# One maximum reduction per head over three key blocks in the causal attention stage

## The chip, the cores and the metric

The kernel runs on one core of a Trainium2 chip. Its time is the device time of the whole program in microseconds (us); a lower time is better. PE is the matrix engine, PEld its weight loads, DVE the vector engine, ACT the scalar engine, POOL the GpSimd engine and SP the engine that issues most transfers.

## The reference

The program applies eight layers to x of shape 16 x 256 x 256 in float32. Each is preceded by a layer norm and added to x. The change touches one of them, the causal self-attention inside the layer L2_ffn, with 16 heads of 16 columns each:

```python
def attention(x, c_attn_w, c_proj_w):
    b, t, c = x.shape
    hd = c // H                       # H = 16, hd = 16
    q, k, v = jnp.split(x @ c_attn_w, 3, axis=-1)
    ...
    att = jnp.einsum('bhqd,bhkd->bhqk', q, k) / jnp.sqrt(jnp.asarray(hd, x.dtype))
    causal = jnp.tril(jnp.ones((t, t), bool))
    att = jnp.where(causal, att, jnp.asarray(-jnp.inf, att.dtype))
    att = jax.nn.softmax(att, axis=-1)
    y = jnp.einsum('bhqk,bhkd->bhqd', att, v)
    y = y.transpose(0, 2, 1, 3).reshape(b, t, c)
    return y @ c_proj_w
...
x = x + attention(layernorm(x, ln1_w), c_attn_w, c_proj_w)
x = x + moe_mlp(layernorm(x, ln2_w), router_w, w1, w2)
```

The softmax needs the maximum over keys of each query of each head. For 256 queries in two tiles of 128, the first tile sees the first 128 keys only, the second all 256. That is three blocks of 128 x 128 scores.

## The kernel before, in words

The function `attention` is called for five attention layers. A call works on 16 units, one batch element of 256 tokens each; the call named a2 holds two layers, first a cross attention (units 0 to 15, a2 in the trace) and behind it the causal self-attention (units 16 to 31, also named a2 in the trace). `stage(u).causal` tells them apart. The tokens, queries, keys and values of several units are in flight at once. A table made by `plan()` gives the order of work for all engines: each period has 16 slots, one for each head, and every engine walks the same table, `PLAN`, and does its own part of each entry. Engines wait for each other by semaphores (`S[name]`).

In slot i of a period, entry `sst` (line 901) makes PE compute the scores of head i of one unit, queries on partitions (`scores`, line 854), into score bank `i % 2`, and interleaved with it the transposed scores of a head of an older unit (`scoresT`, line 866) into one of three other banks. For the causal layer, `diagonal` (line 878) then adds a large negative triangle to the two diagonal blocks. A causal head's scores lie as three adjacent blocks of 128 columns in its bank: queries 0 to 127 against keys 0 to 127, queries 128 to 255 against keys 0 to 127, queries 128 to 255 against keys 128 to 255.

DVE reads the bank and writes the negated maximum of each query into one column of the tile NM (lines 1183 to 1199). For a layer without the causal mask that is one reduction with two outputs (line 1196). For the causal layer there are two reductions a head (line 1193), over 128 and over 256 columns. The second raises the signal `s_max`. PE waits before the scores of head i for `s_max` of head i - 2 (line 907), since there are two score banks. At the change from one unit to the next this goes on: the first head of a unit waits for head 14 of the one before.

In slot 1 of the next period, entry `maxT` (line 979) waits for `s_max` of all 16 heads and transposes the two halves of NM; ACT and DVE split the result into two bfloat16 parts (lines 1110 and 1300), which SP moves into rows of the query tile, so that the transposed scores come out with the maximum subtracted. ACT then takes the exponential (line 1061), and PE multiplies by the values (line 1002).

Between the reductions DVE also does, by the same table: layer-norm statistics (line 1248), the low bfloat16 parts of K and Q (line 1296), the division by the softmax sums (lines 1312 and 1322), the low part of the output (line 1325), the addition to the layer's result (line 1339), and, in the causal units, the router of the following mixture-of-experts layer (statistics at lines 136 to 145, a copy of logits at line 213, the selection at lines 228 to 302 once for each group of units).

Of the kernel before, what the change touches and what calls it, by code (L numbers as in the profile page):

```python
# [4 lines left out]
P = 128  # L5
D = 256
BATCH = 16
SEQ = 256
# [13 lines left out]
F32 = mybir.dt.float32  # L22
# [4 lines left out]
AX = mybir.AxisListType  # L27
ADD, SUB, MUL, MAX, MIN = ALU.add, ALU.subtract, ALU.mult, ALU.max, ALU.min
# [288 lines left out]
def late(u):  # L317
# [3 lines left out]


ATT = ["stats_step", "var_ready", "rstd_ready", "norm_step", "xh_ready", "xs_ready", "ch_ready", "cs_ready", "xT_ps", "xT_sb", "cT_ps", "cT_sb",
       "q_ps", "q_hi", "q_lo", "k_ps", "k_full", "k_hi", "k_lo", "mask_row", "v_ps", "v_sb", "s_ps", "s_max",
       "mT_ps", "m_hi", "m_lo", "st_ps", "p_ready", "pv_ps", "pv_sb", "oT_ps", "recip", "o_ready",
       "o2T_ps", "o2_hi", "o2_lo", "y_ps", "x_done", "x_biased",
       "x_half", "x_joined", "fin_step", "fin_var", "fin_rstd", "fin_n", "fin_max"]
# [13 lines left out]
def attention(nc, g, S, cfg):  # L341

    NH, DH = cfg["heads"], D // cfg["heads"] if "dh" not in cfg else cfg["dh"]
# [11 lines left out]
    stages = [Stage(cfg)] + ([Stage(cfg["then"])] if "then" in cfg else [])  # L355
# [8 lines left out]
    def stage(u):  # L364
        return stages[u // BATCH]
# [8 lines left out]
               k_lo=NB, v_ps=NB, v_sb=NB, s_ps=NH, s_max=NH, st_ps=NH, p_ready=NH,  # L374
# [135 lines left out]
    with ExitStack() as ctx:  # L510
        def sb(name, shape, dt):
            return ctx.enter_context(nc.sbuf_tensor(cfg["name"] + name, shape, dt))
# [10 lines left out]
        QS = sb("QS", [P, RING, CH, GH, SEQ], BF16)  # L523
        KS = sb("KS", [P, RING, CH, GH, SEQ], BF16)
        VA = sb("VA", [P, VRING, 2, NH, VW], F32)
        NM = sb("NM", [P, 2, 2, P], F32)
        MKI = sb("MKI", [P, BATCH * SEQ], I32) if mask else None

        VECS = [sb("VEC%d" % n, [P, 8 + 3 * CK], F32) for n in range(NP_)]
# [67 lines left out]
        with nc.Block() as block:  # L597
# [224 lines left out]
            def _(pe):  # L822
# [64 lines left out]
                for name, u, i, b, before in PLAN:  # L887
# [58 lines left out]
                    elif name in ("q", "k"):  # L946
                        p = u // BATCH
# [29 lines left out]
                                           [wv[:, x, kt, :] for x in range(2)]) for kt in range(KT)])  # L977
                        m.then_inc(S["v_ps"].sem, 1)
                    elif name == "maxT":
                        pe.wait_ge(S["s_max"].sem, S["s_max"].at(u, NH))  # L980
                        take(before)
                        for t in range(2):
                            m = nc.tensor.transpose(misc[:, t * P:t * P + P], NM[:, u % 2, t, :], ident[:])
                        m.then_inc(S["mT_ps"].sem, 1)
                    elif name == "pv":
                        pe.wait_ge(S["p_ready"].sem, S["p_ready"].at(u, (i + 1) * HS))
                        pe.wait_ge(S["v_sb"].sem, S["v_sb"].at(u, NB))
                        take(before)
                        causal = stage(u).causal
                        for t in range(2):  # L990
                            q0 = P if causal and t == 1 else 0
                            for j in range(HS):
                                h = i * HS + j
                                slot = order(h) % 8
                                if wide:
                                    a = (t * HS + j) * W
                                    for kt in range(2):
                                        m = nc.tensor.matmul(misc[:, a:a + VW],
                                                             PT[:, slot, kt * SEQ + t * P:kt * SEQ + t * P + P],
                                                             VA[:, u % VRING, kt, h, :], start=(kt == 0), stop=(kt == 1))  # L1000
                                else:
                                    m = nc.tensor.matmul(misc[32 * j:32 * j + 32, q0:SEQ], VA[:, u % VRING, t, h, :],
                                                         PT[:, slot, t * SEQ:t * SEQ + SEQ - q0],
                                                         start=(t == 0), stop=(t == 1 or causal),
                                                         skip_group_check=causal, tile_position=(0, 32 * j))
                        m.then_inc(S["pv_ps"].sem, 1)
                    elif name == "oT":
                        pe.wait_ge(S["pv_sb"].sem, S["pv_sb"].at(u, (i + 1) * 4 // NO))
                        take(before)
                        for t in range(2):  # L1010
                            for k in range(2):
                                m = nc.tensor.transpose(misc[:, t * 256 + k * P:t * 256 + k * P + P],
                                                        OS[:, 2 * i + k, t * P:t * P + P], ident[:])
                        m.then_inc(S["oT_ps"].sem, 1)
                    elif name == "o2T":
                        pe.wait_ge(S["o_ready"].sem, S["o_ready"].at(u, NO))
                        take(before)
                        for j in range(2):
                            kt = 2 * i + j
                            for t in range(2):  # L1020
                                m = nc.tensor.transpose(misc[:, j * 256 + t * P:j * 256 + t * P + P],
                                                        O[:, t, kt * P:kt * P + P], ident[:])
                        m.then_inc(S["o2T_ps"].sem, 1)
                    elif name == "y" and proj:
                        pe.wait_ge(S["o2_hi"].sem, S["o2_hi"].at(u, NB))
                        pe.wait_ge(S["o2_lo"].sem, S["o2_lo"].at(u, NB))
                        take(before)
                        wo = wos[u // BATCH]
                        for t in range(2):
                            out = misc[:, t * 256:t * 256 + 256]  # L1030
                            m = product3(out, [([oT[:, x, kt, t * P:t * P + P] for x in range(2)],
                                            [wo[:, x, kt, :] for x in range(2)]) for kt in range(CK)])
                        m.then_inc(S["y_ps"].sem, 1)
# [93 lines left out]
            def _(dve):  # L1127
# [32 lines left out]
                for name, u, i, b, before in PLAN:  # L1160
# [22 lines left out]
                    elif name == "sst" and u is not None:  # L1183
# [5 lines left out]
                        col = i if wide else 8 * (i % 2) + i // 2  # L1189
                        bank = ps[:, i % 2, :]  # L1190
                        if stage(u).causal:
                            for t, (lo, hi) in enumerate(((0, P), (P, P + SEQ))):
                                s_ = nc.vector.tensor_reduce(NM[:, u % 2, t, col:col + 1], bank[:, lo:hi],  # L1193
                                                             AX.X, MAX, negate=True)
                        else:
                            s_ = nc.vector.tensor_reduce(NM[:, u % 2, :, col:col + 1],  # L1196
                                                         bank.rearrange("p (t k) -> p t k", t=2),
                                                         AX.X, MAX, negate=True)
                        s_.then_inc(S["s_max"].sem, 1)
                    elif name == "fin":  # L1200
                        step, h = S["fin_step"], u % 2
                        if u == 0:
# [3 lines left out]
                        for t in range(2):  # L1206
                            s_ = nc.vector.bn_stats(FS6[:, t, :], X[:, 2 * u + t, :])
# [3 lines left out]
                        for t in range(2):  # L1211
                            s_ = nc.vector.bn_aggr(FMV[:, h, t, :], FS6[:, t, :])
# [8 lines left out]
                    elif name == "joined":  # L1221
                        WT = g["WT"]
                        for t in range(2 * u, 2 * u + 2):
                            dve.wait_ge(g["gathered"][t % 4], 32 * (t // 4 + 1))
                            s_ = nc.vector.scalar_tensor_tensor(X[:, t, :], GB[:, t % 4, 0, :], WT[:, 0, t:t + 1],
                                                                X[:, t, :], MUL, ADD)
                        s_.then_inc(S["x_half"].sem, 1)
                        dve.wait_ge(S["x_half"].sem, S["x_half"].at(u, 1))
                        for t in range(2 * u, 2 * u + 2):
                            s_ = nc.vector.scalar_tensor_tensor(X[:, t, :], GB[:, t % 4, 1, :], WT[:, 1, t:t + 1],  # L1230
                                                                X[:, t, :], MUL, ADD)
# [122 lines left out]

def signal_used(n, cfg, q, own_ctx, wide):
    proj, mask, self_att = cfg.get("proj"), cfg.get("mask"), q.self_att
    if n in ("q_moved", "q_sent"):
        return (n == "q_sent") == bool(cfg.get("router"))
    if n in ("o2T_ps", "o2_hi", "o2_lo", "y_ps"):
        return bool(proj)  # L1360
    if n in ("pv_sb", "oT_ps"):
        return not wide
    if n in ("k_full", "mask_row"):
        return bool(mask)
    if n in ("ctx_in0", "ctx_in1"):
        return not self_att
    if n in ("cT_ps", "cT_sb", "ch_ready", "cs_ready"):
        return own_ctx
    if n in ("cT_kept0", "cT_kept1"):
        return cfg.get("keep") is not None  # L1370
    if n in ("fin_step", "fin_var", "fin_rstd", "fin_n", "fin_max"):
        return bool(cfg.get("fin"))
    if n == "x_biased":
        return q.biased
    if n in ("x_half", "x_joined"):
        return bool(cfg.get("gather"))
    return True
# [1182 lines left out]
```

## Time and profile before

| | us |
|---|---|
| median of 3 runs | 3309.73 |
| lowest and highest of them | 3307.66, 3317.76 |
| the profiled execution's own time | 3314.98 |
| its span, first to last instruction | 3313.2 |
| TensorE clock granted, mean over the span | 0.921 of full |

The span belongs to one execution. A row of the trace gives the start or the count, the duration, the engine, the source line and the operation as out<-in with the shapes (partitions x elements). What stands in brackets is the idle time of the engine just before, and what ended it. Busy times of PE include a modelled end of each matmul.

### The profile page before, as it was taken

How to read it: one execution, taken by the hardware profiler on the slowest of the kernel's cores; microseconds unless marked ns; L12 is line 12 of the kernel's file. 1: busy time of each engine (PE TensorE's matmuls, PEld its weight loads, DVE VectorE, ACT ScalarE, POOL GpSimd, SP SyncE). 2: the span in 40 equal slices, each digit the busy share in tenths (PEclk: the TensorE clock that was granted, in tenths of full speed). 3: DMA queues.
4: the chain of work that ended last, by engine and by line, in shares of the span. 5: the costliest groups of instructions: out<-in, count | busy, mean ns of one | idle time of the engine just before them, and what ended most of it. 6: DMA issues, size and time to landing. Idle time of an engine off the chain costs nothing. (4 is left out here: it accounts for less than half of the span.)

```text
span 3313.2 us, 69870 instructions
## 1 busy us (share of the span) xinstructions
PE 2813.2 (85%) x25966; PEld 1896.0 (57%) x26085; DVE 1984.3 (60%) x4625; ACT 1663.2 (50%) x3058; POOL 1137.0 (34%) x1192
## 2 busy tenths in 40 slices
PE   4999686888789999999969999998469958999993
PEld 2554463555346666666635556666269936676672
DVE  4887555888455433433358887787554345555547
ACT  2778342777444444444427776766355513333332
POOL 6653008887000000000043334464400064565513
PEclk8999896999779999999969999999789968999995
DMA  3332002222214000000011211111243233332301
GB/s 115 74 74 60 14 5 90 66 67 68 45 53 147 1 1 1 1 1 1 1 60 58 74 47 51 41 61 56 81 143 97 84 100 79 81 83 63 77 20 51
DMA packets 164743, 189.87 MB, mean 57 GB/s; under 512 B 25968, under 2 KB 136832, under 8 KB 164256
## 3 DMA queue, kind: packets, MB, share of 16 engines
q1 hardware_dynamic: 147520, 143.44, 14.5%
q0 software_dynamic: 16896, 41.97, 4.9%
q8 instruction: 218, 3.57, 0.5%
q14 instruction: 109, 0.89, 0.1%
HBM read 67.09 MB, written 41.42 MB: 33 GB/s over the span
## 5 line engine op out<-in xcount | busy, mean ns | idle before, releaser
L1900 DVE TENSOR_TENSOR f1H<-f1HF,f1H 128x512 bf16<-128x512 f32 x256 | 176.6, 692 | 398.3 <-ACT f1H L1740 398.3
L1695 PE MATMUL ps<-f1w,f1H 128*128 128x256 bf16 x3072 | 379.1, 274 | 0.0
L1673 PE MATMUL ps<-f1xT,f1w 128*128 128x512 bf16 x1448 | 360.3, 384 | 12.1 <-ACT f1H L1740 5.9
L1695 PEld LDWEIGHTS ps<-f1w,f1H 128*128 128x128 bf16 x3072 | 301.8, 98 | 90.8 <-issue 1.7
L1737 ACT ACTIVATE f1HF<-ps 128x512 f32<-128x512 f32 x256 | 152.8, 597 | 333.9 <-PE ps L1673 333.8
L1061 ACT ACTIVATE a2PT<-ps 128x512 f32<-128x512 f32 (+1 forms) x512 | 260.1, 542 | 81.7 <-PE ps L884 58.7
L1673 PEld LDWEIGHTS ps<-f1xT,f1w 128*128 128x128 bf16 x1536 | 148.5, 99 | 152.5 <-issue 18.8
L861 PE MATMUL ps<-a2KS,a2QS 49*128 49x256 bf16 (+1 forms) x1024 | 175.9, 267 | 53.9 <-DVE a2NM L1196 20.9
L1583 POOL TENSOR_TENSOR f1RS<-f1VE,neghalf 128x4 f32<-128x4 f32 x8 | 8.1, 1011 | 578.0 <-DVE f1VE L1883 578.0
L1196 DVE TENSOR_REDUCE a0NM<-ps 128x2 f32<-128x512 f32 x256 | 165.5, 685 | 38.2 <-PE ps L861 37.6
L1196 DVE TENSOR_REDUCE a1NM<-ps 128x2 f32<-128x512 f32 x256 | 165.7, 686 | 37.5 <-PE ps L861 35.9
L1196 DVE TENSOR_REDUCE a2NM<-ps 128x2 f32<-128x512 f32 x256 | 165.7, 686 | 27.7 <-PE ps L861 26.0
L873 PE MATMUL ps<-a2QS,a2KS 51*128 51x256 bf16 (+1 forms) x1024 | 173.2, 264 | 0.2 <-ACT a2PT L1061 0.2
L1061 ACT ACTIVATE a4PT<-ps 128x512 f32<-128x512 f32 x128 | 76.0, 597 | 191.6 <-PE ps L873 191.6
L1193 DVE TENSOR_REDUCE a2NM<-ps 128x1 f32<-128x128 f32 (+1 forms) x512 | 150.4, 350 | 31.1 <-PE ps L884 29.8
L1061 ACT ACTIVATE a1PT<-ps 128x512 f32<-128x512 f32 x256 | 143.0, 595 | 25.3 <-PE ps L873 23.7
L805 POOL DMA_INDIRECT Y<-results,IX x64 | 63.4, 990 | 264.6 <-DMA results<-f2OB 247.5
L861 PEld LDWEIGHTS ps<-a2KS,a2QS 49*128 49x128 bf16 x1024 | 67.3, 95 | 147.3 <-DVE a2NM L1196 48.7
L1740 ACT ACTIVATE f1H<-ps 128x512 bf16<-128x512 f32 x256 | 151.5, 592 | 0.0
L1061 ACT ACTIVATE a0PT<-ps 128x512 f32<-128x512 f32 x256 | 141.5, 593 | 16.9 <-PE ps L873 13.6
L861 PE MATMUL ps<-a4KS,a4QS 128*128 128x256 bf16 (+1 forms) x512 | 126.9, 283 | 17.4 <-DMA a4QS<-a4QH 17.4
L733 POOL TENSOR_TENSOR a2RS<-a2VE,neghalf 128x4 f32<-128x4 f32 x32 | 32.7, 1021 | 310.1 <-DVE a2VE L1267 310.1
(538 smaller groups left out, 7046.0 us busy)
## 6 DMA issues: line engine op xcount, KB each, us to landing
a2KS<-a2KH SPq DMA_DIRECT2D x192, 64.0 KB
a2QS<-a2QH SPq DMA_DIRECT2D x192, 64.0 KB
a4KS<-a4KH SPq DMA_DIRECT2D x96, 128.0 KB
a4QS<-a4QH POOLq DMA_DIRECT2D x96, 128.0 KB, 4.3
slots<-zeros SPq DMA_DIRECT2D x1, 9984.0 KB, 31.9
f2XG<-slots SPq DMA_DIRECT2D x39, 256.0 KB, 2.9
results<-f2OB SPq DMA_DIRECT2D x39, 256.0 KB, 2.1
f1WF<-in_f_w SPq DMA_DIRECT2D x32, 256.0 KB, 2.7
```

The source lines that it names most:

```text
L733: nc.gpsimd.tensor_tensor(RS[:, h], VE[:, h], g["neghalf"][:, 0:4], ALU.pow).then_inc(S["rstd_ready"].sem, 1)
L805: nc.gpsimd.indirect_dma_start(GB[:, t % 4, k, :], None, g["results"][:, :], bass.IndirectOffsetOnAxis(ap=g["IX"][:, k, t:t + 1], axis=0)) ...
L861: m = nc.tensor.matmul(bank[:, at:at + keys], QS[r0:r1, u % RING, ch, gi, t * P:t * P + P], KS[r0:r1, u % RING, ch, gi, 0:keys], start=(ch ...
L873: m = nc.tensor.matmul(bank[:, at:at + SEQ - q0], KS[r0:r1, u % RING, ch, gi, t * P:t * P + P], QS[r0:r1, u % RING, ch, gi, q0:SEQ], start ...
L1061: nc.scalar.activation(PT[:, ic % 8, 0:n_], ps[:, 2 + (uc * NH + ic) % 3, 0:n_], ACT.Exp, scale=scale).then_inc(S["p_ready"].sem, 1)
L1193: s_ = nc.vector.tensor_reduce(NM[:, u % 2, t, col:col + 1], bank[:, lo:hi], AX.X, MAX, negate=True)
L1196: s_ = nc.vector.tensor_reduce(NM[:, u % 2, :, col:col + 1], bank.rearrange("p (t k) -> p t k", t=2), AX.X, MAX, negate=True)
L1673: m = nc.tensor.matmul(ps[:, (u * NCH + i) % 2, :], w1[:, x, kt, i * P:i * P + P], xT[:, half, y, kt, :], start=(j == 0), stop=(j == len(t ...
L1695: m = nc.tensor.matmul(out, H[:, (u * NCH + i) % HR, x, t * P:t * P + P], w2[:, y, i, :], start=first, stop=(f == YC - 1 and j == 2 and no ...
L1737: nc.scalar.activation(HF[:, (u * NCH + i) % 2, :], ps[:, (u * NCH + i) % 2, :], cfg["gelu"], **bias).then_inc(S["h_full"].sem, 1)
L1740: nc.scalar.activation(H[:, (u * NCH + i) % HR, 0, :], ps[:, (u * NCH + i) % 2, :], cfg["gelu"], **bias).then_inc(S["h_hi"].sem, 1)
L1900: nc.vector.tensor_tensor(H[:, (u * NCH + i) % HR, 1, :], HF[:, (u * NCH + i) % 2, :], H[:, (u * NCH + i) % HR, 0, :], SUB).then_inc(S["h_ ...
```

## The change

In the causal layer one reduction a head now covers the three blocks of 128 columns and writes three outputs, so NM has three blocks instead of two in the call a2. After the last head of a unit, DVE waits for its own reductions and takes the elementwise minimum of the blocks 1 and 2 (of negated maxima, 128 x 16) into block 1, and raises a new signal `m_full`. PE's `maxT` waits for `m_full` instead of `s_max` in the causal layer. The reduction of the other layers is the same as before, written with an explicit `0:2`.

```diff
-        NM = sb("NM", [P, 2, 2, P], F32)
+        NM = sb("NM", [P, 2, 3 if any(q.causal for q in stages) else 2, P], F32)
...
                     elif name == "maxT":
-                        pe.wait_ge(S["s_max"].sem, S["s_max"].at(u, NH))
+                        if stage(u).causal:
+                            pe.wait_ge(S["m_full"].sem, S["m_full"].at(u % BATCH, 1))
+                        else:
+                            pe.wait_ge(S["s_max"].sem, S["s_max"].at(u, NH))
...
                         if stage(u).causal:
-                            for t, (lo, hi) in enumerate(((0, P), (P, P + SEQ))):
-                                s_ = nc.vector.tensor_reduce(NM[:, u % 2, t, col:col + 1], bank[:, lo:hi],
-                                                             AX.X, MAX, negate=True)
+                            s_ = nc.vector.tensor_reduce(NM[:, u % 2, :, col:col + 1],
+                                                         bank[:, 0:3 * P].rearrange("p (b k) -> p b k", b=3),
+                                                         AX.X, MAX, negate=True)
                         else:
-                            s_ = nc.vector.tensor_reduce(NM[:, u % 2, :, col:col + 1],
+                            s_ = nc.vector.tensor_reduce(NM[:, u % 2, 0:2, col:col + 1],
                                                          bank.rearrange("p (t k) -> p t k", t=2),
                                                          AX.X, MAX, negate=True)
                         s_.then_inc(S["s_max"].sem, 1)
+                        if stage(u).causal and i == NH - 1:
+
+                            dve.wait_ge(S["s_max"].sem, S["s_max"].at(u, NH))
+                            nc.vector.tensor_tensor(NM[:, u % 2, 1, 0:NH], NM[:, u % 2, 1, 0:NH], NM[:, u % 2, 2, 0:NH], MIN
+                                                    ).then_inc(S["m_full"].sem, 1)
```

The name `m_full` is also added to the list `ATT`, and `signal_used` returns `q.causal` for it.

On DVE, at the change from one causal unit to the next in a period with the router's copy of logits, the order before was (a2oT is the low part of the output, f2G the router's logits; the four reductions are heads 14 and 15, the two behind the copy are head 0 of the next unit):

```order
L1325 TENSOR_TENSOR a2oT<-ps,a2oT 128x512
L1193 TENSOR_REDUCE a2NM<-ps 128x1 x4
L213 COPY f2G<-ps 128x16
L1193 TENSOR_REDUCE a2NM<-ps 128x1 x2
L1248 BN_STATS a2ST<-X 128x6 x2
```

and with the change it is:

```order
L1333 TENSOR_TENSOR a2oT<-ps,a2oT 128x512
L1195 TENSOR_REDUCE a2NM<-ps 128x3 x2
L1206 TENSOR_TENSOR a2NM<-a2NM 128x16
L213 COPY f2G<-ps 128x16
L1195 TENSOR_REDUCE a2NM<-ps 128x3
L1256 BN_STATS a2ST<-X 128x6 x2
```

The minimum (line 1206) stands between head 15 and the copy of logits, and so ahead of head 0 of the next unit; each pair of reductions is one.

On PE, at entry `maxT` of a causal unit, with the signals that each row waits for, the order before was:

```order
L884 MATMUL ps<-tri_t,idh 128x2x128
L983 MATMUL ps<-ident,a2NM 128x128 [waits r_gc,s_max]
L983 MATMUL ps<-ident,a2NM 128x128
L1002 MATMUL ps<-a2PT,a2VA 32x256 [waits xT_sb,v_sb,p_ready]
```

and with the change:

```order
L884 MATMUL ps<-tri_t,idh 128x2x128
L986 MATMUL ps<-ident,a2NM 128x128 [waits r_gc,m_full]
L986 MATMUL ps<-ident,a2NM 128x128
L1005 MATMUL ps<-a2PT,a2VA 32x256 [waits xT_sb,v_sb,p_ready]
```

PE's rows keep their places; only the signal before the transposes differs.

## Rows read from the trace of the kernel before

**Rows 1.** The page, busy time of each engine over the whole span.

```profile
PE 2813.2 (85%) x25966; PEld 1896.0 (57%) x26085; DVE 1984.3 (60%) x4625; ACT 1663.2 (50%) x3058; POOL 1137.0 (34%) x1192
```

**Rows 2.** Busy times by stretch: PE, PEld, DVE, ACT, POOL, clock, DMA share, GB/s.

```profile
1999.00:2325.00 326.00, 302.19 (x4359) 213.49 (x4359) 257.42 (x886) 218.00 (x448) 172.07 (x167) 0.97 0.16 52
```

**Rows 3.** Table of waits from 1999 to 2325: us in total, times, longest.

```profile
PEld ps L861 <- DVE a2NM L1193: 32.0, 86, 2.1
...
PE ps L861 <- DVE a2NM L1193: 15.2, 24, 1.8
```

**Rows 4.** Timeline of weight loads: start, us, operation, idle before and its releaser.

```profile
2083.38 0.09 PEld L861 LDWEIGHTS ps<-a2KS,a2QS 49*128 49x128 bf16 x1 [0.62 <-DVE a2NM L1193]
...
2008.21 0.09 PEld L861 LDWEIGHTS ps<-a2KS,a2QS 49*128 49x128 bf16 x1 [0.41 <-DVE a2NM L1193]
...
2087.32 0.09 PEld L861 LDWEIGHTS ps<-a2KS,a2QS 49*128 49x128 bf16 x1 [0.20 <-issue]
```

**Rows 5.** Timeline of DVE in a steady causal unit.

```profile
2080.34 0.69 DVE L1296 TENSOR_TENSOR a2KH<-ps,a2KH 128x512 bf16<-128x512 f32 x1 [1.19 <-ACT a2KH L1094]
...
2082.71 1.14 DVE L1193 TENSOR_REDUCE a2NM<-ps 128x1 f32<-128x128 f32 x4
2083.77 0.68 DVE L1296 TENSOR_TENSOR a2QH<-ps,a2QH 128x512 bf16<-128x512 f32 x1
```

**Rows 6.** DVE by line and shape: count, busy us, mean ns, idle before.

```profile
L1193 DVE TENSOR_REDUCE a2NM<-ps 128x1 f32<-128x256 f32 x256 | 106.2, 415 | 0.0
L1193 DVE TENSOR_REDUCE a2NM<-ps 128x1 f32<-128x128 f32 x256 | 72.8, 285 | 31.1 <-PE ps L884 29.8 <-issue 0.4
...
L1196 DVE TENSOR_REDUCE a2NM<-ps 128x2 f32<-128x512 f32 x256 | 165.7, 686 | 27.7 <-PE ps L861 26.0
...
L232 DVE TENSOR_REDUCE f2RK<-a2WF 128x64 f32<-128x512 f32 x2 | 1.4, 686 | 0.1
```

**Rows 7.** Timeline of DVE late in the cross-attention units, two heads in a row.

```profile
1993.61 1.29 DVE L1196 TENSOR_REDUCE a2NM<-ps 128x2 f32<-128x512 f32 x2 [0.26 <-PE ps L861]
1994.81 0.25 DVE L1312 RECIPROCAL a2RC<-ps 128x16 f32<-128x16 f32 x1
```

**Rows 8.** Timeline of DVE around the router's selection, and in the last period.

```profile
2160.35 0.61 DVE L1193 TENSOR_REDUCE a2NM<-ps 128x1 f32<-128x128 f32 x2
...
2172.01 0.17 DVE L301 TENSOR_TENSOR f2AB<-f2AB 128x8 f32<-128x8 f32 x1
2172.21 0.17 DVE L302 CAST IX<-f2AB 128x16 int32<-128x16 f32 x1
2172.29 1.15 DVE L1193 TENSOR_REDUCE a2NM<-ps 128x1 f32<-128x128 f32 x4
...
2315.59 3.59 DVE L1193 TENSOR_REDUCE a2NM<-ps 128x1 f32<-128x128 f32 x12
```

**Rows 9.** Timeline of DVE, a dependent pair of statistics and a small product.

```profile
2095.23 0.25 DVE L1257 BATCH_NORM_AGGREGATE a2MV<-a2ST 128x2 f32<-128x6 f32 x2 [0.17 <-DVE a2ST L1248]
...
2096.84 0.41 DVE L1302 TENSOR_TENSOR a2MH<-ps,a2MH 16x256 bf16<-16x256 f32 x1
```

**Rows 10.** Timeline of DVE and of weight loads at a change of causal units.

```profile
2092.32 1.14 DVE L1193 TENSOR_REDUCE a2NM<-ps 128x1 f32<-128x128 f32 x4
...
2093.78 0.62 DVE L1193 TENSOR_REDUCE a2NM<-ps 128x1 f32<-128x128 f32 x2 [0.24 <-PE ps L884]
...
2095.92 0.20 PEld L983 LDWEIGHTS ps<-ident,a2NM 128*128 128x128 f32 x2 [0.16 <-issue]
```

**Rows 11.** Line 721, POOL's clearing of NM: ns min/median/max, start.

```profile
L721 POOL MEMSET a2NM<- x1: 519/519/519, 1667.5 to 1667.5; 128x512 f32 x1
```

**Rows 12.** Busy times by stretch behind the router's selection, columns as in Rows 2.

```profile
2165.00:2170.00 5.00, 2.48 (x30) 1.71 (x32) 4.62 (x23) 1.69 (x4) 1.62 (x2) 1.00 0.24 81
2170.00:2175.00 5.00, 3.91 (x51) 2.58 (x52) 4.36 (x19) 2.35 (x5) 1.47 (x2) 0.65 0.15 52
2175.00:2180.00 5.00, 5.00 (x61) 3.33 (x61) 2.62 (x8) 2.88 (x5) 3.33 (x4) 0.67 0.30 103
```

More of the change, by code:

```diff
@@ L323 @@
 ATT = ["stats_step", "var_ready", "rstd_ready", "norm_step", "xh_ready", "xs_ready", "ch_ready", "cs_ready", "xT_ps", "xT_sb", "cT_ps", "cT_sb",
-       "q_ps", "q_hi", "q_lo", "k_ps", "k_full", "k_hi", "k_lo", "mask_row", "v_ps", "v_sb", "s_ps", "s_max",
+       "q_ps", "q_hi", "q_lo", "k_ps", "k_full", "k_hi", "k_lo", "mask_row", "v_ps", "v_sb", "s_ps", "s_max", "m_full",
        "mT_ps", "m_hi", "m_lo", "st_ps", "p_ready", "pv_ps", "pv_sb", "oT_ps", "recip", "o_ready",
@@ L1356, in signal_used @@
     proj, mask, self_att = cfg.get("proj"), cfg.get("mask"), q.self_att
+    if n == "m_full":
+        return q.causal
     if n in ("q_moved", "q_sent"):
```

## The prediction

> **What bounds the kernel now.** I read the page first: over the whole span PE is busy 85%, DVE 60% [rows 1]. That average says little, since the change touches one stage. The causal units run from 1999 us to 2325 us of the span, and the table by stretches gives that stage alone: PE 302.2 of 326 us (93%), PE's weight loads 65%, DVE 79%, ACT 67% [rows 2]. So PE is nearest to full, with DVE behind it. The table of waits then says how often DVE's maxima hold PE up: matmuls of line 861 sat idle 15.2 us in 24 places for the tile NM, and weight loads of that line 32.0 us in 86 places [rows 3]. Not all of the 32.0 us is loss. After other matmul work line 861 shows a gap of 0.20 us with nothing to wait for the third of [rows 4], and 86 such gaps are 17.2 us; what is really lost to DVE is therefore about 15 us in 326, by both ways of counting. The timeline shows the kinds of place. In a steady unit DVE does the low part of K, a reciprocal, a product and statistics from 2080.34 us on and reaches two waiting score banks only at 2082.71 us [rows 5]; PE, which has two score banks, resumes at 2083.38 us after 0.62 us of idle weight loads [rows 4], 0.06 us after the first head's maxima ended (2082.71 + 0.61). Elsewhere DVE waits for PE.
>
> **What goes and what comes.** 512 reductions go (256 over 128 elements, mean 285 ns, and 256 over 256 elements, mean 415 ns) [rows 6]; 256 reductions over 384 elements and 16 minima of 128x16 come. No matmul, activation, transfer or its order moves. PE's transposes wait for the new signal instead of the maxima.
>
> *One reduction over 384 elements.* No row has it. The two neighbours are 256 elements at 415 ns and 512 elements (two outputs) at 686 ns [rows 6]; halfway is 550 ns. The number of outputs seems free: 64 outputs from 512 elements take 686 ns as well [rows 6]. What counts on a queue is the distance from start to start. Two heads of the old pairs take from 2082.71 to 2083.77 us, 0.53 us a head [rows 5]; two 512-element reductions take from 1993.61 to 1994.81 us, 0.60 us each [rows 7]. A slope of (686 - 415) / 256 = 1.06 ns an element takes 0.135 us off that for 128 fewer elements: 0.465 us a head. The saving is 0.065 us a head, and a head that starts with DVE free is also done about 0.06 us sooner (0.62, the second of [rows 10], to 0.55). Over 256 heads that is 16.6 us of DVE's time. The bounds are the neighbours: at the 512-element price, 0.60, each head costs 0.07 us more than now; at 256 elements, 0.33, each saves 0.20.
>
> The Trainium skill (VectorE: DVE Perf Modes, section on the TRN2 errata) prices a PSUM-source instruction at 120 cycles plus one per element at 0.96 GHz. By that a removed instruction would save 125 ns, 32 us in all on DVE, and a 384-element reduction would take 525 ns. The rows disagree with it about the queue: two back-to-back reductions already overlap, so only about half of that fixed cost comes back.
>
> *The minimum, once a unit.* It waits for its own engine's last reduction. In a chain of dependent small instructions the next starts 0.03 us after the end of the one before, lasts 0.17 us at 128x16, and the following reduction starts 0.08 us after it [rows 8]. To that comes the tail of the reduction that is no longer overlapped, 0.55 - 0.465 = 0.085. Together 0.20 us a unit, 3.2 us of DVE over 16 units. Upper end: the extra 0.17 us that the statistics pair shows between dependent instructions, and 0.41 us, the longest small two-input operation nearby [rows 9]: 0.085 + 0.17 + 0.41 = 0.67 us. Lower end 0.085 us, the lost overlap alone. I take 0.20, since lines 301 and 302 are nearest in kind and size.
>
> On the path it costs nothing. It stands behind the two last heads of a unit (the pair at 2092.32 us); next comes head 0 of the following unit, before which DVE idles 0.24 us for PE [rows 10]. The minimum fits into this and into the 0.13 us that the two heads leave free. The copy of router logits behind it moves by 0.2 us at most, and PE's transposes, which want both it and the minimum, run at 2095.92 us [rows 10], over 2 us later. If that cover went, the price is 0.20 us a unit, 3.2 us.
>
> *The larger NM.* Its clearing on POOL, 519 ns for 512 elements [rows 11], grows to 768 elements: at most 0.26 us more, once. Nothing is waiting for it between 1667.5 us and the causal stage at 1999 us but the block's first unit; uncovered it would cost those 0.26 us. I set it to nothing.
>
> **What reaches the end.** PE gains only where it waits for DVE and DVE has been busy without a pause, and there one 0.065 for each head in that run:
> - ten steady units have the place with two heads (of 2083.38 us): 10 x 0.13 = 1.3 us;
> - two units contain the router's selection, where DVE is busy without a pause from head 2 at 2160.35 us to heads 8 and 9 at 2172.29 us [rows 8]: 8 heads, 0.52 us each, 1.0 us;
> - the last period has no new projections, and DVE does six heads in a row at 2315.59 us [rows 8]; with the head before it 7 heads, 0.45 us;
> - in the first units five waits like the one of 0.41 us at 2008.21 us [rows 4] have one or two heads behind them: 0.45 us;
> - at the change of unit DVE is named in the four earliest units, one head each: 0.25 us.
>
> The sum is 3.5 us. The profiled execution took 3314.98 us, so it would take 3311.5. It was a slow one: the median of the three runs is 3309.73, and the gain is taken from that: 3306.2 us. Where PE no longer waits for DVE it is next held by its own matmuls.
>
> **Rivals.**
>
> *A. DVE sets the stage's pace.* If DVE were behind most of the 86 waits, its whole relief would arrive: 16.6 - 3.2 = 13.4 us, 3296.3 us. For it: those waits, and weight loads at 65% only. Against: DVE idles for PE before heads too, and 15 us is all that PE loses to it; a wait seldom has more than two heads in DVE's run. The Trainium skill (Perfetto Trace Analysis, section on identifying the most-contended engine) says that matmul busy time is no measure of PE's headroom and that weight-load occupancy should be used; by that rule DVE at 79% would be the busier engine in this stage, which is this rival. Chance 0.12.
>
> *B. The minimum lands on the path (slower).* Place: DVE between head 15 and head 0 of the next unit. It decides if minimum and lost overlap pass 0.37 us (the 0.24 of idle and 0.13 saved) or if the idle before head 0 vanishes because PE comes earlier. At the upper price and with no cover, 16 x 0.67 = 10.7 us, less 3.5: 3316.9 us. Against: the dependent pair 301, 302 at a third of that price. Chance 0.05.
>
> *C. The three-block reduction costs as much as the 512-element one.* Then the 54 heads counted above each cost 0.07 us: plus 3.8 us, 3313.5 us. Against: the slope in rows 6 is the same between 128, 256 and 512 elements. Chance 0.07.
>
> *D. PE's granted clock.* After DVE's long run the clock goes to half: PE was busy 2.48 of 5 us from 2165 us, and the grant was 0.67 from 2175 us [rows 12]. With 5 us at 0.65 ahead of that (the stretch from 2170 us), such a dip loses 1.7 + 1.7 = 3.4 us of PE's work. If 0.5 us less waiting avoids one dip, the time is 3302.8; if an earlier or later phase adds one, 3309.6. The level, 0.5 against 1.0, is 1.2 against 2.4 GHz. Chance 0.06.
>
> **The numbers.** The forecast keeps 0.70. A measurement of this kernel can tell about 0.3% (9.9 us) from no change; the three runs span 10 us themselves. The forecast, C and D lie within it, B nearly. A lies outside. Faster by over 0.3%: 0.12 from A and 0.02 from the spread; slower: 0.04, most of B's upper price and spread; within: 0.82. The range takes in C and D, nearly all of A's side and the spread of runs of some 5 us on the other: 3297 to 3315 us.
>
> **What would show it.** In the new profile the reduction's mean should be 0.54 to 0.56 us, two heads in a row 0.93 us from start to start, the minimum 0.16 to 0.20 us, with no new wait before the transposes. DVE's busy time in the stage should fall by some 10 to 20 us while PE's wait for NM falls by 3 to 5 us only, and the stage should last 322 to 323 us instead of 326. A stage under 316 us would make A right; a wait of PE for the minimum, or head 0 starting later against PE, B; a reduction over 0.6 us, C; another count of dips in the clock, D.

## The result and the profile after

| | before | after |
|---|---|---|
| median of 14 runs each, us | 3310.13 | 3304.47 |
| lowest and highest, us | 3305.16, 3318.92 | 3299.85, 3308.07 |
| profiled execution, us | 3314.98 | 3300.47 |
| its span, us | 3313.2 | 3298.6 |

The ratio is 0.9979 with a 95% interval of [0.997, 0.9988]: 5.7 us less in the median, a real gain and under the 0.3% named as the bound. The page of the changed kernel, busy times over the span:

```profile
PE 2800.4 (85%) x26085; PEld 1887.0 (57%) x26085; DVE 1970.3 (60%) x4385; ACT 1661.6 (50%) x3058; POOL 1144.6 (35%) x1192
```

It answers to [rows 1] and says as little. The causal stage is best measured between the split of the maxima (the small product of line 1302, now 1310) of its first and its last unit, 17 such instructions and 16 periods between them. First before, then after, the table by stretches (PE, PEld, DVE, ACT, POOL, clock, DMA share, GB/s):

```profile
2002.14:2327.74 325.60, 301.79 (x4356) 213.09 (x4352) 255.77 (x879) 216.80 (x447) 171.11 (x167) 0.97 0.16 52
```

```profile
1992.01:2309.98 317.97, 294.57 (x4356) 209.38 (x4352) 243.28 (x640) 215.83 (x447) 171.60 (x167) 1.00 0.16 53
```

DVE has 12.5 us less to do. The stage is 7.6 us shorter, and its granted clock has risen from 0.97 to 1.00. The operations themselves, by line and shape (count, busy us, mean ns, idle before):

```profile
L1195 DVE TENSOR_REDUCE a2NM<-ps 128x3 f32<-128x384 f32 x256 | 133.9, 552 | 31.8 <-PE ps L884 28.1 <-issue 1.8
L1206 DVE TENSOR_TENSOR a2NM<-a2NM 128x16 f32<-128x16 f32 x15 | 2.6, 175 | 0.5
```

The reduction takes 552 ns, against the 550 halfway between its neighbours in [rows 6], and the minimum 175 ns. What PE waits for, table of waits of the stage (us in total, times, longest), answers to [rows 3]:

```profile
PEld ps L861 <- DVE a2NM L1195: 26.0, 58, 2.1
...
PE ps L861 <- DVE a2NM L1195: 15.3, 23, 1.8
```

The weight loads wait 6.0 us less and in 28 places fewer, the matmuls as long as before (15.3 against 15.2 us). Most of this is a change of name: with 0.20 us taken off for each place, as the prediction did, 14.8 us were lost before and 14.4 are lost now. So this table does not account for the gain; the places themselves do. The place of [rows 4, 5] in a steady unit, DVE and then weight loads:

```profile
2091.23 1.01 DVE L1195 TENSOR_REDUCE a2NM<-ps 128x3 f32<-128x384 f32 x2
2092.16 0.68 DVE L1304 TENSOR_TENSOR a2QH<-ps,a2QH 128x512 bf16<-128x512 f32 x1
...
2091.83 0.09 PEld L861 LDWEIGHTS ps<-a2KS,a2QS 49*128 49x128 bf16 x1 [0.56 <-DVE a2NM L1195]
2092.29 0.09 PEld L861 LDWEIGHTS ps<-a2KS,a2QS 49*128 49x128 bf16 x1 [0.18 <-DVE a2NM L1195]
```

Two heads take 0.93 us from start to start instead of 1.06, and PE's first gap falls from 0.62 to 0.56 us, the second from 0.25 to 0.18 us, as short as a start for which nothing has to be waited. The change of unit, which answers to [rows 10]:

```profile
2100.70 1.01 DVE L1195 TENSOR_REDUCE a2NM<-ps 128x3 f32<-128x384 f32 x2
2101.75 0.18 DVE L1206 TENSOR_TENSOR a2NM<-a2NM 128x16 f32<-128x16 f32 x1
2101.84 0.17 DVE L213 COPY f2G<-ps 128x16 f32<-128x16 f32 x1
2102.10 0.56 DVE L1195 TENSOR_REDUCE a2NM<-ps 128x3 f32<-128x384 f32 x1
...
2104.25 0.20 PEld L986 LDWEIGHTS ps<-ident,a2NM 128*128 128x128 f32 x2 [0.16 <-issue]
```

The minimum starts 0.04 us after the last reduction's end, the copy 0.09 us later, and DVE is done with both before head 0 starts. PE's transposes come 2.3 us after it without a wait. Just ahead of the minimum PE starts the scores of head 0 of the next unit, for which it needs the bank of head 14. That weight load, before at the place of [rows 10], then after:

```profile
2093.15 0.09 PEld L861 LDWEIGHTS ps<-a2KS,a2QS 49*128 49x128 bf16 x1 [0.53 <-issue]
...
2101.48 0.09 PEld L861 LDWEIGHTS ps<-a2KS,a2QS 49*128 49x128 bf16 x1 [0.47 <-issue]
```

This gap is 0.06 us shorter too, although the trace names no releaser for it. Counted from the unit's product, PE's weight loads are 0.06 us earlier at head 4, 0.13 us from head 5 on, and 0.19 us from this place on.

Period by period, from the starts of those 17 products, the gain has two sizes:

| us | first profile before | first profile after |
|---|---|---|
| a steady unit | 19.72 | 19.53 |
| first selection unit | 28.35 | 26.10 |
| second selection unit | 28.72 | 26.10 |
| all 14 others together | 268.53 | 265.77 |

The selection units are those in which DVE picks the experts' slots [rows 8]. They give 4.9 us of the 7.6, far more than their eight heads can (0.52 us each). The granted clock differs as well. Both stretches, before and after:

```profile
2156.18:2184.53 28.35, 22.25 (x300) 15.38 (x296) 24.25 (x85) 14.62 (x29) 15.98 (x14) 0.88 0.14 48
2244.04:2272.76 28.72, 23.75 (x300) 16.14 (x296) 24.34 (x86) 14.51 (x29) 15.89 (x15) 0.82 0.14 48
```

```profile
2144.23:2170.33 26.10, 19.86 (x300) 13.78 (x296) 23.45 (x69) 14.43 (x29) 16.09 (x14) 1.00 0.16 52
2229.63:2255.73 26.10, 19.86 (x300) 13.79 (x296) 23.44 (x70) 14.38 (x29) 15.99 (x14) 1.00 0.16 53
```

In this execution the clock, which had been at half (1.2 GHz) for part of both units, stayed at 2.4 GHz. Whether that belongs to the change or to this execution was the open question.

### The profile page after: what moved, and what is told of

It reads as the page before. It is cut to its first block and busy times, and to the rows that moved or that the text cites. A ratio compares the mean times of both kernels' runs of the same rounds, so it can differ in the third digit from the quotient of the medians.

```text
span 3298.6 us, 69750 instructions
## 1 busy us (share of the span) xinstructions
PE 2800.4 (85%) x26085; PEld 1887.0 (57%) x26085; DVE 1970.3 (60%) x4385; ACT 1661.6 (50%) x3058; POOL 1144.6 (35%) x1192
## 5 line engine op out<-in xcount | busy, mean ns | idle before, releaser
L1683 PE MATMUL ps<-f1xT,f1w 128*128 128x512 bf16 x1536 | 378.5, 383 | 5.9 <-ACT f1H L1750 5.9
L1195 DVE TENSOR_REDUCE a2NM<-ps 128x3 f32<-128x384 f32 x256 | 133.9, 552 | 31.8 <-PE ps L884 28.1
L1064 ACT ACTIVATE a0PT<-ps 128x512 f32<-128x512 f32 x256 | 141.4, 593 | 15.8 <-PE ps L873 12.5
```

Of the source, the lines that this page charges most:

```text
L1064: nc.scalar.activation(PT[:, ic % 8, 0:n_], ps[:, 2 + (uc * NH + ic) % 3, 0:n_], ACT.Exp, scale=scale).then_inc(S["p_ready"].sem, 1)
L1195: s_ = nc.vector.tensor_reduce(NM[:, u % 2, :, col:col + 1], bank[:, 0:3 * P].rearrange("p (b k) -> p b k", b=3), AX.X, MAX, negate=True)
L1683: m = nc.tensor.matmul(ps[:, (u * NCH + i) % 2, :], w1[:, x, kt, i * P:i * P + P], xT[:, half, y, kt, :], start=(j == 0), stop=(j == len(t ...
```

## The experiments

Two theories stood after the result. Theory 1 is that of the prediction: PE gains only behind a run of DVE without a pause, 0.065 us a head. Theory 2: the rest comes from TensorE's clock. The rival to the first is still that DVE's total sets the pace. Each ratio below is against runs of the kernel before on the same chip.

### The changed kernel again, and both kernels profiled four times

No edit.

> The changed kernel once more, unaltered, for the spread and for the clock. Theory 1 (sites: PE gains only where it waits for DVE behind a run of reductions without a pause, 0.065 us a head): a steady unit lasts 19.53 us as in the first profile (before: 19.72), the ratio to before lies between 0.997 and 0.999. Theory 2 (clock: about half of the gain is that TensorE's clock no longer falls behind the router's selection, where the first profile of the changed kernel has 26.1 us a unit and before had 28.3 and 28.7): both selection units again last about 26.1 us and the stage again shows a granted clock of 1.00. If the clock falls only by chance of the execution, one of them is near 28 us this time.

> The kernel before the change, unaltered, against itself: ratio 1 within 0.002. Steady units 19.72 us again by theory 1. By theory 2 (the clock falls behind the router's selection because PE idles long enough there) both selection units are again 28 us or more, with a granted clock under 1 in them. If the fall is a matter of chance, one of them is near 26.6 us (26.1 of the changed kernel and 8 heads of 0.065).

> A third profile of the kernel before, for how often the clock falls in the causal stage: theory 2 in its strict form says 28 us or more in both selection units, chance says one near 26.6.

> A third profile of the changed kernel: strict theory 2 says a clock of 1.00 through the causal stage and 26.1 us in both selection units; chance says that a fall of the clock shows here at least once.

> A fourth profile of the kernel before. So far its two selection units lasted 28.4 and 28.7, 28.6 and 27.7, 28.4 and 27.7 us, each with a fall of the clock. If the change shifts how often the clock falls, they are both over 27.5 us again; if the earlier difference to the changed kernel was luck, one is near 26.5 us.

> A fourth profile of the changed kernel. Five of its six selection units so far lasted 26.1 us and one 28.1. If the change shifts how often the clock falls, at least one of the two is at 26.1 us; if it was luck, both are over 27.5 us as in the kernel before.

The changed kernel had a ratio of 0.9975 [0.9964, 0.9987] (median 3306.31 us), the kernel before against itself 0.9997 [0.9988, 1.0006]. The four profiles of each:

| us | stage | selection units | the 14 others |
|---|---|---|---|
| before, 1 | 325.60 | 28.35, 28.72 | 268.53 |
| before, 2 | 324.57 | 28.57, 27.74 | 268.26 |
| before, 3 | 324.62 | 28.38, 27.69 | 268.55 |
| before, 4 | 324.44 | 28.60, 27.81 | 268.03 |
| mean | 324.8 | 28.2 | 268.3 |
| after, 1 | 317.97 | 26.10, 26.10 | 265.77 |
| after, 2 | 317.81 | 26.10, 26.09 | 265.62 |
| after, 3 | 320.19 | 28.11, 26.10 | 265.98 |
| after, 4 | 319.71 | 28.29, 26.09 | 265.33 |
| mean | 318.9 | 26.6 | 265.7 |

The means differ by 5.9 us, close to the 5.7 of the medians; the first pair of profiles overstated it. The closeness is in part luck: the whole spans of the four profiles differ by 9.6 us in the mean, of which 3.7 lie ahead of the stage and behind it. The strict form of theory 2 falls: the clock does fall in the changed kernel too. After, profile 3, whole stage and both selection units:

```profile
1997.45:2317.64 320.19, 298.23 (x4356) 211.78 (x4352) 243.38 (x640) 216.24 (x447) 171.54 (x167) 0.98 0.16 53
2150.29:2178.40 28.11, 22.15 (x300) 15.54 (x296) 23.63 (x69) 14.57 (x29) 16.07 (x14) 0.88 0.15 49
2237.27:2263.37 26.10, 21.22 (x300) 14.49 (x296) 23.45 (x70) 14.30 (x29) 15.98 (x14) 0.93 0.16 53
```

Before, profile 4, the same stretches:

```profile
2004.21:2328.65 324.44, 302.11 (x4356) 213.09 (x4352) 255.33 (x878) 216.47 (x447) 171.39 (x167) 0.97 0.16 52
2158.03:2186.63 28.60, 23.69 (x300) 16.08 (x296) 24.23 (x86) 14.51 (x29) 16.00 (x14) 0.82 0.14 48
2245.88:2273.69 27.81, 22.63 (x300) 15.36 (x296) 24.22 (x85) 14.36 (x29) 15.91 (x14) 0.88 0.15 50
```

The grant is under 1 in 8 of 8 selection units before and in 3 of 8 after, and one of those three cost nothing (the 26.10 at 0.93). The other two cost 2.0 and 2.2 us. So in these profiles a fall costs time in eight units of eight before and in two of eight after. Units with the same granted clock give the part of the reductions alone: at 0.88 the first selection unit lasted 28.35 and 28.38 us before and 28.11 after, at 0.82 it lasted 28.57 and 28.60 before and 28.29 after, 0.3 us less each time.

That the rarer falls belong to the change is not shown. The eight units are four executions, and the two units of one are not independent: four of four executions lost time before, two of four after. The edits that follow make it weaker still. The kernel without the minimum, the larger and the smaller reduction and the moved statistics have a fall in each of their eight selection units, though three of the four give DVE no more work than the changed kernel. The granted clock over whole executions leans towards fewer falls: 0.9239 in 34 executions of the kernel before and 0.9247 in 11 of the changed kernel on the same chip, with standard errors of 0.0003 and 0.0005. A difference of 0.001 stands for some 3 us of PE's time (an estimate, 0.001 of the span), so these means do not settle it either. For something beyond the reductions speak the times: the two intervals of the ratio are 4.0 to 9.9 us and 4.3 to 11.9 us, both above the 3.5 us of the reductions, the first only just.

### Without the minimum

```diff
-                        if stage(u).causal and i == NH - 1:
-                            dve.wait_ge(S["s_max"].sem, S["s_max"].at(u, NH))
-                            nc.vector.tensor_tensor(NM[:, u % 2, 1, 0:NH], ...)
...
-                            pe.wait_ge(S["m_full"].sem, S["m_full"].at(u % BATCH, 1))
+                            pe.wait_ge(S["s_max"].sem, S["s_max"].at(u, NH))
```

The maximum of queries 128 to 255 then leaves out keys 128 to 255.

> The changed kernel without the minimum: the maximum of queries 128 to 255 then covers keys 0 to 127 only, PE's transposes wait for the reductions as before the change. Theory 1 with the minimum hidden in DVE's idle time: the same time as the changed kernel within 1 us, a steady unit 19.53 us. Rival (the minimum lies on the path at 0.2 us a unit): 3 us less than the changed kernel, a steady unit 19.33 us.

Ratio 0.9972 [0.996, 0.9985]; the changed kernel beside it had 0.9975, 1 us more. The medians, 3302.13 and 3306.31 us, differ by 4.2 us, and taken alone they would rather speak for the rival; with intervals of 4 us to either side the times cannot decide. The trace can. A steady unit lasts 19.53 us in both, the selection units 26.41 and 26.57 (clock 0.94 in both). So by the steady units the minimum is off the path, to 0.01 us, where the rival wanted 19.33.

### A larger and a smaller reduction

```diff
-    s_ = nc.vector.tensor_reduce(NM[:, u % 2, :, col:col + 1],
-                                 bank[:, 0:3 * P].rearrange("p (b k) -> p b k", b=3),
+    s_ = nc.vector.tensor_reduce(NM[:, u % 2, 0:2, col:col + 1],
+                                 bank.rearrange("p (t k) -> p t k", t=2),
```

> The changed kernel with a reduction over all 512 columns of the bank in two outputs of 256 instead of 384 in three; the maxima then cover other queries' columns too, so that the subtracted shift differs. DVE has 0.135 us more for each head, 34.6 us over the stage. Theory 1: only the heads behind which PE waits count, three in a steady unit: 19.9 us a steady unit, 26.1 + 1.1 = 27.2 us a selection unit, in all 8 to 12 us more than the changed kernel and 2 to 6 us more than before. Rival (DVE sets the pace everywhere): 30 us more than the changed kernel, a steady unit 21.6 us.

Ratio 1.001 [1.0, 1.0021], median 3314.37 us, 8.1 us more than the changed kernel beside it and 0.5 more than the kernel before, where 2 to 6 were expected; by the ratio it is 3. The stage lasts 328.75 us, 9.9 more than the mean of the changed kernel; theory 1 gave 8 to 12, the rival 30. The steady unit is 19.96 us (19.9 expected, 21.6 by the rival), the selection units 28.28 both (27.2 expected; the clock fell in both). The place in a steady unit, DVE and weight loads:

```profile
2097.06 1.28 DVE L1195 TENSOR_REDUCE a2NM<-ps 128x2 f32<-128x512 f32 x2
2098.26 0.68 DVE L1304 TENSOR_TENSOR a2QH<-ps,a2QH 128x512 bf16<-128x512 f32 x1
...
2097.79 0.09 PEld L861 LDWEIGHTS ps<-a2KS,a2QS 49*128 49x128 bf16 x1 [0.72 <-DVE a2NM L1195]
2098.39 0.09 PEld L861 LDWEIGHTS ps<-a2KS,a2QS 49*128 49x128 bf16 x1 [0.32 <-DVE a2NM L1195]
```

Against the changed kernel each head adds 0.135 us: PE's second start is 0.60 us behind the first instead of 0.46. 34.6 us more of DVE's time became 8 to 10 us of the program's, so the rest was slack.

The smaller one takes `bank[:, 0:2 * P]` with `b=2` and so leaves out the third block.

> The changed kernel with the reduction cut to the first 256 columns in two outputs (the third block of each head, keys 128 to 255 of the later queries, is left out of the maximum). DVE has 0.135 us less a head, 34.6 us over the stage. Theory 1: a steady unit gains for at most three heads, 0.2 to 0.4 us (19.15 to 19.35 us), selection units 1 us each, in all 4 to 7 us less than the changed kernel. Rival (DVE sets the pace): 30 us less, a steady unit 17.4 us.

Ratio 0.9956 [0.9942, 0.9969]; the stage lasts 312.77 us, 6.1 less than the changed kernel's mean, a steady unit 19.14 us, the selection units 26.55 and 25.49 (25.1 expected; the clock fell in both). Theory 1 gave 4 to 7 us, the rival 30. One slope in both directions: 0.4 us a steady unit for 0.135 us a head, which is three heads. The place at the change of unit follows it: PE's gap there is 0.60 us in the larger one, 0.47 in the changed kernel and 0.34 in the smaller one (where one unit shows 0.67 behind a transfer).

### The router's statistics elsewhere

```diff
-            put(3, "r_stats", "n", 0)
...
+        if router:
+            put(13, "r_stats", "n", 0)
```

> The changed kernel with the router's statistics (two BN_STATS, two BN_AGGR, one small operation, together 1.1 us of DVE a unit) moved from slot 3 of the period to slot 13, where DVE waits 0.9 us for ACT. Theory 1: the wait of PE for head 4 (weight loads idle 0.6 us) is made by DVE's other work in front of it and goes, 0.3 to 0.45 us a steady unit, some 4 to 6 us less than the changed kernel, of which the later place may take 1 to 2 back. Rival (DVE's total sets the pace): no change, since DVE's work is the same.

A steady unit falls to 19.15 us. PE's wait for head 4 is gone; DVE and weight loads at that place:

```profile
2097.83 0.42 DVE L1331 TENSOR_TENSOR a2O<-ps,a2RC 128x256 f32<-128x256 f32 x1
2098.18 1.01 DVE L1196 TENSOR_REDUCE a2NM<-ps 128x3 f32<-128x384 f32 x2
...
2099.56 0.09 PEld L862 LDWEIGHTS ps<-a2KS,a2QS 49*128 49x128 bf16 x1 [0.20 <-issue]
```

DVE's work is the same in sum and only stands elsewhere, so it was the run in front of the head that cost, not DVE's total. The 14 periods outside the selection last 261.0 us, 4.7 less than the mean of the changed kernel. The ratio, 0.9973 [0.9961, 0.9985], is that of the changed kernel all the same. The expected 4 to 6 us did not arrive in the whole: both selection units lasted 27.94 us with the clock at 0.88, 3.7 us more than the 26.10 twice. What remains of the gain in this profile's stage (316.88 us against a mean of 318.9) is 2.0 us.

### The selection cut into pieces

The functions of the selection become generators that stop between operations, and the table calls them in more slots:

```diff
-            put(1, "r_choose", "l", 0)
-            put(3, "r_rank", "l", 0)
-            put(5, "r_runs", "l", 0)
-            put(7, "r_places", "l", 0)
+            for k, n in ((1, "r_choose"), (2, "r_choose"), (3, "r_choose"), (5, "r_rank"), (6, "r_runs"), (7, "r_runs"),
+                         (8, "r_runs"), (9, "r_places"), (10, "r_places")):
+                put(k, n, "l", 0)
...
-                if router and k == 9:
+                if router and k == 12:
...
+        yield
```

> The changed kernel with the router's selection on DVE cut into eight pieces with the maxima of a head between them (choose in slots 1 to 3, the ranks in 5, runs in 6 to 8, places in 9 and 10, scatters after slot 12 instead of 9). Theory 1 (PE waits for DVE behind runs without a pause): the selection unit falls from 26.1 to about the busy time of DVE in it, 23.5 to 25 us, no PE wait for the maxima over 1 us. Theory 2 (the clock falls because PE idles long enough in that unit): the clock no longer falls there in any execution, so that on top of 2 x 1.5 us the loss by the clock goes: 3 to 5 us less than the changed kernel in the median. If the clock falls for another reason, falls of the clock stay as they were.

> The cut selection and the router's statistics in slot 13 together. Steady units 19.15 us as with the statistics moved alone, selection units 23.5 to 25 us. If both gains add, 7 to 9 us less than the changed kernel and 12 to 15 us less than before (ratio about 0.996); if moving the statistics is what let the clock fall in the earlier run (27.9 us in both selection units), the falls are back and the time is that of the cut selection alone.

Cut alone, the selection units last 24.67 and 25.60 us, and the stage 315.28. The two stretches:

```profile
2144.80:2169.47 24.67, 19.66 (x300) 13.88 (x296) 22.77 (x70) 14.50 (x29) 15.58 (x14) 1.00 0.17 56
2228.06:2253.66 25.60, 21.14 (x300) 14.74 (x296) 22.76 (x69) 14.61 (x29) 15.51 (x14) 0.93 0.16 54
```

The waits of PE for NM inside that first unit shrink; the table of waits, first the changed kernel, then this one:

```profile
PEld ps L861 <- DVE a2NM L1195: 5.6, 7, 2.1
PE ps L861 <- DVE a2NM L1195: 4.0, 3, 1.8
```

```profile
PEld ps L865 <- DVE a2NM L1207: 3.8, 5, 1.3
PE ps L865 <- DVE a2NM L1207: 2.6, 4, 1.1
```

The longest is 1.3 us, not under 1 us as expected. The clock still fell in one of the two units. And the ratio, 0.9982 [0.9972, 0.9991], shows nothing of the 3.6 us of the stage. Part of it seems to be given back behind the stage: from the last product to the end the span has 991.0 us here, and 984.7, 985.0, 988.6 and 988.9 in the four profiles of the changed kernel. And the profiled execution, 3300.51 us, is 6.5 us under the median of its 12, 3307.00, so its stage need not be that of the others. The rest is within the interval.

Both edits together have the lowest ratio of the versions that keep the whole computation: median 3300.79 us, ratio 0.9964 [0.9952, 0.9976], 10.9 us under the kernel before on that chip, where 12 to 15 were expected. The interval still overlaps that of the changed kernel, 0.9975 [0.9964, 0.9987]. The stage lasts 309.53 us, 9.4 less than the changed kernel's mean (7 to 9 expected), a steady unit 19.15. The stage and its selection units:

```profile
1998.75:2308.28 309.53, 292.20 (x4356) 210.00 (x4352) 241.58 (x640) 215.26 (x447) 170.84 (x167) 1.00 0.17 55
2149.71:2173.95 24.24, 19.82 (x300) 13.82 (x296) 22.78 (x70) 14.62 (x29) 15.71 (x14) 1.00 0.17 56
2231.38:2255.63 24.25, 19.82 (x300) 13.82 (x296) 22.79 (x69) 14.62 (x29) 15.58 (x14) 1.00 0.17 57
```

Here both gains arrive in the stage and the clock holds. So the moved statistics do not by themselves bring the falls back; what brought them in the run before this one stays open.

## Why the prediction was right

Forecast 3306.2 us in 3297 to 3315; measured 3304.47. The gain was 5.7 us where 3.5 were forecast. The time alone tests little, since the range holds the unchanged median, 3310.13 us, as well. What was right is the mechanism of the reductions and its size. The other 2 us or so came from a term that the sum had at nothing, and two misses inside the sum cancelled, which was luck.

- **The reduction's price.** Forecast 550 ns alone and 0.465 us from start to start; measured 552 ns and 0.93 us for two. The Trainium skill (VectorE: DVE Perf Modes, section on the TRN2 errata) would have it at 525 ns and at 125 ns saved for each instruction removed; by the rows it is 0.065 us. The measurement decides for the overlap.
- **The minimum.** Forecast 0.20 us a unit, hidden. It lasts 0.175 us, and leaving it out changed a steady unit by nothing. Rival B is out.
- **Steady units.** Two heads were counted, 0.13 us; measured 0.19, so three. The third is head 14, for which PE waits at the change of unit (0.53 us before, 0.47 after). The prediction gave that place to the four earliest units only, since the trace names ACT or nothing as the releaser in the others. The slopes of the larger and smaller reductions count three as well.
- **The 14 periods outside the selection.** The terms 1.3, 0.45, 0.45 and 0.25 sum to 2.45 us; the means give 2.7: 1.6 in the steady units, 0.75 in the first four (0.70 forecast) and 0.3 in the last period. The steady units do not give ten times 0.19, because the one behind the first selection unit gains nothing.
- **PE's wait for NM.** A fall of 3 to 5 us was to show it; the weight loads' fell by 6.0 us and the matmuls' not at all. The deduction of 0.20 us a place, which gave "about 15 us" as PE's loss, gives 14.4 after, so it did not measure what the change could save.
- **The selection units.** 0.52 us each was too much. In the first profiles heads 8 and 9 start 16.11 us after the unit's product before and 15.91 after, 0.20 us for six heads' worth. The saving of heads 2 and 3 is lost, since an operation of line 145 in front of head 4 lasts 1.15 us instead of 1.08 and ends at the same place; only the four heads behind it count. With heads 8 and 9 and the head at the change of unit some 0.4 us a unit are the reductions' (an estimate at 0.065 a head); units of equal granted clock show 0.3. That is 0.6 to 0.8 in all.
- **The clock.** This term was missing from the sum and stood as rival D with a chance of 0.06. Of the 3.2 us that the selection units gave on average, 0.6 to 0.8 are the reductions', so some 2.5 us came from the clock in these profiles. Rival D had the place right and the price too high: 3.4 us were allowed for a fall, and it cost 2.0 and 2.2 in the changed kernel. Its chance was put too low if the change is the reason; if the executions merely differed, the extra gain was luck. The record leaves both standing.
- **Rival A** is out: PE is the stage's bound, DVE's total is not. With 34.6 us added or taken, the stage moved by 9.9 and 6.1. The Trainium skill's rule (Perfetto Trace Analysis, section on identifying the most-contended engine) pointed to DVE here, 79% against 65% of weight loads, and it would have given 13.4 us; PE's matmul occupancy of 93% was the better guide in this stage.
- **Rival C** is out by the measured 552 ns.

The sum therefore stands at 3.3 to 3.5 us for the reductions (2.7 and 0.6 to 0.8), where 3.5 were forecast, and some 2.5 us for the clock, together the 5.9 of the stage. What stays open is why the fall became rarer, and whether it did at all. The two kernels differ in that unit by a few tenths of a microsecond of PE's idle time, and cutting the selection made PE's waits shorter while a fall still came in one of four such units.

## What to carry to other kernels

The worth of a cheaper operation on an engine that is not the bound is its saving times the number of such operations that stand, without a pause, between the bound's last release and its next: count them in one steady unit and multiply. The engine's total, here 12.5 us less, is only the ceiling. When a few long runs of small work make PE wait, look at the granted clock in the same stretch over several executions before and after; here it carried nearly as much of the difference between the profiles as the operation itself. One profile on each side can mislead (7.6 us where the means gave 5.9), and four are too few to say whether the change or the execution moved the clock.

## What the hardware showed beyond that

- Two reductions back to back from PSUM overlap by 0.085 us (552 ns alone, 0.465 from start to start), and so do those of 512 (686 and 0.60) and the pairs of 128 and 256. The number of outputs hardly counts: 256 elements take 415 ns with one output and 420 ns with two, and 512 take 686 ns with 2 or 64.
- The same kernel on the same data had its clock at half for part of a selection unit in one execution and not in another. The 14 runs of the changed kernel lie over 8 us, with mean clocks from 0.923 to 0.929, and the higher clocks go with the shorter times (correlation -0.8).
- An operation on 128x2 elements (line 145), 0.17 us in steady units, lasts 1.1 us in the first selection unit. In both first profiles it ended 0.02 us after an operation of POOL (line 749, 1.16 us) that had started up to 0.1 us before it. Whether the one held up the other was not tried.
